# Two expert layers of a perceiver block: totals kept by adding scatters, the shared expert inside routing, the choice in halves

## What is computed

```
# layer 0: E=64 experts, K=6 of them for a token, hidden width 176
s = softmax(x @ gate_w.T); idx = the K largest of s + gate_b; w = s[idx]
# an expert takes its first CAP=128 tokens in token order; later ones are dropped
y[tok] += w * (silu(x[tok] @ w1.T) * (x[tok] @ w3.T)) @ w2.T
y += (silu(x @ ws1.T) * (x @ ws3.T)) @ ws2.T          # shared expert, width 352

# layer 1: 64 experts, TOPK=8 from the best 4 of 8 groups, hidden width 128, no cap
s = sigmoid(x @ w_router); swb = s + b_router
# group score = sum of its two largest swb; swb of other groups is set to 0
idx = the 8 largest; w = 2.5 * s[idx] / (sum(s[idx]) + 1e-20)
y[tok] += w * (silu(x[tok] @ we_gate) * (x[tok] @ we_up)) @ we_down
y += (silu(x @ ws_gate) * (x @ ws_up)) @ ws_down      # shared expert, width 128
```

## Time and profile before

| | us |
|---|---|
| median of 3 runs | 2524.7 (2523.28 to 2529.2) |
| profiled execution | 2530.89 |
| its span | 2529.0 |

### The profile page before, as it was taken

The page is one execution under the profiler, slowest core; times in us unless marked ns, Lnnn a source line. Parts: engine busy times, 40 slices in busy tenths (PEclk is TensorE's granted clock), DMA queues, the critical chain, the costliest instruction groups (busy, mean ns, idle before and its releaser), DMA issues. The chain is left out here.

```text
span 2529.0 us, 40086 instructions
## 1 busy us (share of the span) xinstructions
PE 1946.5 (77%) x11338; PEld 1327.9 (53%) x11339; DVE 1596.9 (63%) x3459; ACT 1052.6 (42%) x3039; POOL 1204.2 (48%) x999
## 2 busy tenths in 40 slices
PE   5699967888887646998868999778635899998410
PEld 5378833343433232775436888567521777776200
DVE  6599818999999867334846777455579333332643
ACT  1367627656574234442027777433215222222000
POOL 1488606766666501774004555255300544453576
PEclk9699988999999955999969999899855899999755
DMA  7211213303030012885421111000040889899333
GB/s 214 79 67 74 99 33 133 108 27 121 14 134 1 0 59 77 264 253 159 126 67 31 35 31 31 27 2 1 26 154 1 255 277 275 276 260 225 104 115 106
DMA packets 163386, 274.38 MB, mean 108 GB/s; under 512 B 28674, under 2 KB 95339, under 8 KB 163060
## 3 DMA queue, kind: packets, MB, share of 16 engines
q1 hardware_dynamic: 108788, 186.31, 23.4%
q0 software_dynamic: 24320, 58.81, 8.9%
q10 hardware_dynamic: 30144, 27.62, 3.2%
HBM read 223.03 MB, written 56.90 MB: 111 GB/s over the span
## 5 line engine op out<-in xcount | busy, mean ns | idle before, releaser
L982 POOL TENSOR_TENSOR b_h<-b_h,b_bcb 128x1024 f32<-128x1024 f32 x128 | 301.8, 2358 | 151.4 <-DVE b_h L1020 150.8
L1406 POOL DMA_INDIRECT m1x_xb<-scratch_xn,m_tok x192 | 181.5, 945 | 334.9 <-PE m1x_psx L1433 166.9
L838 PE MATMUL b_psy<-b_h,ident 128*128 128x512 f32 x512 | 255.0, 625 | 75.2 <-POOL b_h L982 75.1
L1020 DVE TENSOR_TENSOR_SCAN b_h<-b_dA,b_pbx 128x1024 f32<-128x1024 f32 x128 | 292.6, 2286 | 4.4
L1504 DVE TENSOR_TENSOR m1x_hT<-m1x_sg,m1x_psh 128x128 f32<-128x128 f32 x192 | 55.3, 288 | 260.0 <-ACT m1x_sg L1475 260.0
L1444 PE MATMUL m1x_psh<-m1x_xe,m1x_w 128*128 128x128 f32 x1536 | 209.3, 280 | 10.7 <-DMA m1x_w<-in_m_w 10.6
L838 PEld LDWEIGHTS b_psy<-b_h,ident 128*128 128x128 f32 x512 | 94.7, 196 | 218.8 <-POOL b_h L982 130.4
L940 ACT ACTIVATE b_dA<-b_delta,b_A 128x504 f32<-128x504 f32 x256 | 166.8, 706 | 92.9 <-DVE b_h L1020 88.0
L1444 PEld LDWEIGHTS m1x_psh<-m1x_xe,m1x_w 128*128 128x128 f32 x1536 | 190.3, 195 | 15.4 <-DMA m1x_w<-in_m_w 7.2
L1014 DVE TENSOR_TENSOR b_pbx<-b_pdx,b_bcb 128x1024 f32<-128x1024 f32 x128 | 157.6, 1231 | 51.1 <-ACT b_pdx L924 45.1
L1768 POOL TENSOR_TENSOR x_s<-x_s,x_rs 128x1024 f32<-128x1024 f32 x64 | 121.1, 1893 | 133.7 <-DVE x_rs L1935 133.6
(11 more groups left out here) (421 smaller groups left out, 4590.4 us busy)
## 6 DMA issues: line engine op xcount, KB each, us to landing
m1x_w<-in_m_w SPq DMA_DIRECT2D x192, 256.0 KB, 4.4
b_bcb<-scratch_bc_rows SPq DMA_DIRECT2D x64, 512.0 KB, 4.8
scratch_y<-m1x_yb ACTq DMA_DIRECT2D x192, 128.0 KB, 4.2
m0x_w<-in_m_w SPq DMA_DIRECT2D x64, 368.0 KB
scratch_y<-a_clear SPq DMA_DIRECT2D x16, 768.0 KB, 3.2
m0c_yg<-scratch_y SPq DMA_DIRECT2D x16, 768.0 KB, 4.6
a_c<-in_ctxT SPq DMA_DIRECT2D x16, 512.0 KB, 3.7
m0x_w<-in_m_w SPq DMA_DIRECT2D x64, 128.0 KB
```

Source lines behind the costliest of these rows:

```text
L838: mm = pe.matmul(psy[:, k % 2, :], ident[:, :], h[:, u % HB, j, :], start=False, stop=(nq == NQ - 1 and j == CQ - 1))
L982: q.tensor_tensor(hs, hs, bcb[:, 1, CQ * nq:CQ * nq + CQ], ALU.mult).then_inc(sem("hc"), 1)
L1020: v.tensor_tensor_scan(h[:, u % HB].rearrange("p j n -> p (j n)"), dA[:, u % DB].rearrange("p j n -> p (j n)"), pbx[:, :, :].rearrange("p ...
L1406: g.indirect_dma_start(out=xb[:, j, :], out_offset=None, in_=xn, in_offset=bass.IndirectOffsetOnAxis(ap=tok[:, b:b + 1], axis=0)).then_inc ...
```

## The change

Layer 0: the scores are stored behind each row of `xn` (rows of 320 numbers), so that a gathered row carries its token's weights. DVE multiplies a block's output by the row's score for that expert. Instead of a row for each token and choice there are three totals of one row a token (`NSUM` = 3, with 128 spare rows for empty slots); POOL's scatter of block b adds into total b mod 3, and waits until that total's last scatter has landed. The combine adds three totals for four tiles at a time. The first stage clears 6.7 MB in 6 stores. R becomes 16, and the first 16 blocks' weights are loaded during routing. The table carries only the token, DVE writes `atb` for one pair in three, ACT for two.

Both layers: normalized tiles go through a ring of 4, ACT copies a turned tile once, gate products stay in PSUM for all tiles. The choice (`chosen`) is made for 8 tiles and then for the other 8. Units 0 to `SECOND` - 1 of the shared expert (7 of 12, 4 of 4) are computed in routing, the rest in combine. POOL's gather waits for the output of the block R before.

```diff
-    R = 8
+    totals = [d[f"y{layer}{n}"] for n in range(NSUM)] if capped else None
+    R, XR = 16 if capped else 8, 4
+    UNITS = NSB * NG
+    FIRST, SECOND = (2, 7) if capped else (2, 4)
...
+        def shared_products(pe, m, gate, up):
+            g, n = m // NSB, m % NSB
+            for k2, out in enumerate((gate, up)):
+                for k in range(KD):
+                    mm = pe.matmul(out[0:SBW[n]], ws13[:, k, k2, P * n:P * n + SBW[n]], xnT[:, k, GT * g:GT * g + GT],
+                                   start=(k == 0), stop=(k == KD - 1))
+            mm.then_inc(rs("gu"), 1)
+        def shared_gated(v, m, up):
+            g, n = m // NSB, m % NSB
+            w = SBW[n]
+            v.wait_ge(rs("sgs"), m + 1)
+            v.tensor_tensor(hs[0:w, n, GT * g:GT * g + GT], sgs[0:w, m % 2, :], up[0:w], ALU.mult).then_inc(rs("hs"), 1)
...
             def by_scalar(n):
-                return capped or n % ACT3 == ACT3 - 1
+                return n % 3 != 2 if capped else n % 3 == 2
...
+                    for t in range(NT):
+                        sp.wait_ge(rs("xr"), t + 1)
+                        sp.dma_start(xn[P * t:P * t + P, 0:D], xr[:, t % XR, :]).then_inc(rs("xr_stored", t % XR), 16)
+                    if capped:
+                        for j in range(R):
+                            expert_weights(sp, j, j)
+                    else:
+                        sp.dma_start(w2all[:, :, :], d["m1_w2"].rearrange("e f d -> f e d")).then_inc(rs("w2all"), 16)
+                    if capped:
+                        sp.wait_ge(rs("scores"), 2)
+                        sp.dma_start(xn[:, D:D + E].rearrange("(t p) e -> p t e", p=P), sc[:, :, :]).then_inc(rs("scores_stored"), 16)
...
+                    turn(0)
+                    for t in range(1, NT):
+                        turn(t)
+                        logits(t - 1)
+                    logits(NT - 1)
+                    for m in range(FIRST):
+                        units(m)
+                    pe.wait_ge(rs("hs"), FIRST)
+                    for n in range(2):
+                        for k in range(K):
+                            pe.wait_ge(rs("oh"), K * n + k + 1)
+                            for ranks, w in ((psl, ltrib), (pst, onesb)):
+                                mm = pe.matmul(ranks[:, HN * n:HN * n + HN, :], w[:, :], oh[:, HN * n:HN * n + HN, k, :], start=(k == 0), stop=(k == K - 1))
                     mm.then_inc(rs("ranks"), 1)
+                    for m in range(FIRST, SECOND):
+                        units(m)
...
+                    for t in range(XR, NT):
+                        normed(t)
+                    chosen(0)
+                    chosen(1)
...
+                    shared_gated(v, FIRST, gate_up(FIRST)[1])
+                    for n in range(2):
+                        q = slice(HN * n, HN * n + HN)
+                        for k in range(K):
+                            ins = v.tensor_tensor(pr[:, :, k, :], oh[:, q, k, :], sel[:, q, :], ALU.mult)
+                        step(ins)
+                        step(v.tensor_reduce(slotf[:, q, :], pr[:, :, :, :], AX_X, ALU.add))
+                        for m in range(FIRST + 1 + 2 * n, min(FIRST + 3 + 2 * n, SECOND)):
+                            shared_gated(v, m, gate_up(m)[1])
...
+                    step(v.tensor_scalar(tok[:, :], table, -1.0, 0.0, ALU.add, ALU.max))
+                    step(v.tensor_scalar(slotv[:, 0, :], table, 0.0, nodest[:, 0:1], ALU.is_equal, ALU.mult))
+                    step(v.scalar_tensor_tensor(dest[:, :], slotv[:, 0, :], -1.0, table, ALU.add, ALU.add))
...
                     def rows(b):
                         j, n = b % R, b // R
                         if n:
-                            g.wait_ge(xs("xb", j), 16 * n)
-                            g.wait_ge(xs("xb_used", j), n)
+                            g.wait_ge(xs("yb", b % 2), (b - R) // 2 + 1)
+                            if capped:
+                                g.wait_ge(xs("y_added", (b - R) % NSUM), 16 * ((b - R) // NSUM + 1))
...
                     def outputs(b):
-                        j, n = b % R, b // R
+                        s, n = b % NSUM, b // NSUM
                         g.wait_ge(xs("yb", b % 2), b // 2 + 1)
-                        g.indirect_dma_start(out=y, out_offset=bass.IndirectOffsetOnAxis(ap=dest[:, b:b + 1], axis=0), in_=yb[:, j, :],
-                                             in_offset=None, bounds_check=T * K - 1, oob_is_err=False).then_inc(xs("y_stored", j), 16)
+                        if n:
+                            g.wait_ge(xs("y_added", s), 16 * n)
+                        g.indirect_dma_start(out=totals[s], out_offset=bass.IndirectOffsetOnAxis(ap=dest[:, b:b + 1], axis=0), in_=yb[:, b % R, :],
+                                             in_offset=None, compute_op=ALU.add).then_inc(xs("y_added", s), 16)
...
+                            v.tensor_scalar(yb[:, j, :], psyy[u][:, 0:D], xb[:, j, bass.ds(R * p + j + D, 1)], None, ALU.mult).then_inc(xs("yb", u), 1)
...
+                    for g in range(NG) if capped else ():
+                        for s in range(NSUM):
+                            sp.dma_start(yg[:, g, s, :, :], totals[s].rearrange("(t p) d -> p t d", p=P)[:, 4 * g:4 * g + 4, :]).then_inc(cs("yg", g), 16)
...
+                        v.wait_ge(cs("yg", g), 16 * NSUM)
+                        for s in range(NSUM):
+                            v.tensor_tensor(xg, xg, yg[:, g, s, :, :], ALU.add).then_inc(cs("summed"), 1)
+                            v.wait_ge(cs("summed"), NSUM * g + s + 1)
+                        for i in range(t - 3, t + 1) if capped else ():
+                            v.bn_stats(e["stats"][:, i, :], X[:, i, :]).then_inc(cs("next_bn"), 1)
```

More of the change, by code:

```diff
@@ L44 @@
 HB0 = 64
-SLOTS0 = E * CAP0
 NB1 = T * K1 // P + E
-SLOTS1 = NB1 * P
+NSUM = 3
 HK = 16
@@ L247, in stage_mla @@
         oT = sb("oT", [P, 2, 8, P])
-        NCL = 16
-        clear = sb("clear", [P, T * K0 * D // (P * NCL)])
-        y_clear = d["y0"].rearrange("(n p r) d -> n p (r d)", n=NCL, p=P)
+        NCL = 2
+        clear = sb("clear", [P, (T + P) * D // (P * NCL)])
+        y_clear = [d[f"y{layer}{n}"].rearrange("t d -> (t d)").rearrange("(m p f) -> m p f", m=NCL, p=P)[m]
+                   for layer in range(1) for n in range(NSUM) for m in range(NCL)]
         psk = ps("psk", [P, 4, 512])
@@ L1112, in stage_moe @@
             atb = r.sb("atb", [P, HQ, NA], F16)
[L1113 to L1117, removed]
+            psT = [r.ps(f"psT{n}", [P, 512]) for n in range(2)]
             psl = r.ps("psl", [P, NT, E])
@@ L1167, in _ @@
[L1167 to L1173, removed]
+                            mm = pe.matmul(psc[:, t, :], xnT[:, k, P * t:P * t + P], gw[:, k, :], start=(k == 0), stop=(k == KD - 1))
@@ new lines, in logits, with units @@
+                        mm.then_inc(rs("logits"), 1)
+                    def units(m):
+                        pe.wait_ge(rs("shared"), 32)
+                        if m > FIRST:
+                            pe.wait_ge(rs("sel"), 1)
+                        if m >= 2 and m != FIRST:
+                            pe.wait_ge(rs("hs"), m - 1)
+                        shared_products(pe, m, *gate_up(m))
+                    turn(0)
+                    for t in range(1, NT):
+                        turn(t)
+                        logits(t - 1)
@@ L1290, in _ @@
-                    for t in range(NT):
-                        ins = v.max(top[:, t, :], sel[:, t, :])
-                    step(ins)
-                    for t in range(NT):
-                        ins = v.max_index(topi[:, t, :], top[:, t, :], sel[:, t, :])
-                    step(ins)
-                    step(v.tensor_copy(topf[:, :, :], topi[:, :, :]))
-                    for k in range(K):
-                        v.tensor_tensor(oh[:, :, k, :], bc(iota[:, None, :], NE), bc(topf[:, :, k:k + 1], NE), ALU.is_equal).then_inc(rs("oh"), 1)
+                    step(v.memset(before[:, 0, :], 0.0))
```

430 lines of the change are left out of this document (208 added, 222 removed).

## The result

The changed kernel takes 2489.5 us (median of 4 runs, 2484.0 to 2490.9), the kernel before 2525.7 beside it. The ratio is 0.9852, 95% interval 0.9832 to 0.9871: 36 us faster. The forecast was 2469, range 2457 to 2506, so the direction and the range hold and the size is 20 us short.

A forecast was written before the change was run, and what follows sets the result against it. Bounds before: PE in both expert loops, DVE in both routings and the first combine, POOL in the last. Terms summed to -55.7 us, 2530.9 to 2475.2 profiled, less 6.2 to the median: 2469, range 2457 to 2506.

The forecast's parts named there:

- The experts of layer 0, the adding scatter: Layer 0 experts: POOL's adding scatter taken at 1.02 us, like a plain one, upper bound 2.0; no cost.
- rival A: Layer 0 experts: POOL becomes the bound through a longer adding scatter, +13 at 1.5 us, +45 at 2.0; chance 0.14.
- B: Layer 0 experts: the three chains of additions pace blocks mildly, landing 8.1 to 10.6 us, +18 at 9; chance 0.15.
- The step to the median, -6.2: Whole kernel: the profiled execution lay 6.2 us above the runs' median; the same difference was taken off 2475.2.
- The landing of the adding scatter, 6.5 taken: Layer 0 experts: an adding scatter lands in 6.5 us, free up to 8.1 with three totals; effect 0.
- C: Layer 0 experts: chains of additions make the kernel slower than before, landing 10.8 us or more, up to +69; chance 0.06.
- Borders of rounds, -1.5: Layer 0 experts: four rounds instead of eight save half of the excess at the borders of rounds, -1.5 us.
- Combine of layer 0, -44.6: Layer 0 combine: less DVE work makes PE the bound, 47.8 us instead of 92.4, -44.6.
- Routing of layer 0, -7.2: Layer 0 routing: shorter table loop -10.0, tail -1.0, gated products +3.3, halves' overhead +0.5; sum -7.2 us.
- Rival D: Routing: shared units stay at 1.2 GHz and DVE waits for them, +11 us in layer 0, +4 in layer 1; chance 0.08.
- Layer 1: Layer 1: routing -1.2 us, bounds -4 and +4; experts 0; combine 0.
- First stages: First stage: 6 clears for 16, behind DVE and PE, 0 us.

The follow-up runs named there:

- e1: The changed kernel with plain scatters in layer 0's experts, the addition in the transfer left out: 2470.8 us, ratio 0.9754.
- e2: The changed kernel with six totals instead of three, the combine reading only three of them: 2491.1 us, ratio 0.9841.
- e8: The changed kernel with each adding scatter taking only rows 0 to 63 of the block's 128: 2497.4 us, ratio 0.9624.
- e12: The kernel before with only layer 0's expert rings changed, 16 blocks in four rounds instead of 8 in eight: 2527.8 us, ratio 0.9994.
- e4: The changed kernel with nine of layer 0's shared units in routing instead of seven, and three gated products after each half's slots instead of two: 2496.0 us, 0.9863.
- e7: The changed kernel with eight shared units in layer 0's expert loop, four in routing, none in combine, gated products regrouped: 2488.9 us, ratio 0.9590.
- e9: The changed kernel with seven shared units in routing, five in layer 0's expert loop, none in combine, gated products regrouped: 2497.1 us, ratio 0.9618.

## Why the prediction was right in direction and 20 us off

*The experts of layer 0, the adding scatter: "I take 1.02".* This is the step that failed: a term mis-sized. The bounds on record were 1.02 and 2.0, the value taken the lower end because of the same 128 rows of 1 KB. It measured 1.58, and with 0.28 us a block to spare that made POOL the bound. This is rival A, priced at 13 us for 1.5 and 45 for 2.0; 1.58 put into the same sum (0.97 + 1.58 + 0.54 = 3.09 a block) gives +18, and the loop came out 17.9 us above the forecast (+16.4 for -1.5). e1 takes the addition out: its loop is 20.2 us shorter, its time 20.3 below e2's on the same chip, and 0.9754 of 2524.7 is 2463, inside the forecast's own range of 2460 to 2478. "The same rows, the same kind" was the wrong argument, since e8 shows that the rows hardly count. The measured time lies outside that range of its own and inside the wide one only because the wide one had been drawn to take in rivals A and B.

*The step to the median, -6.2.* The sum gave 2475.2 for a profiled execution, and that measured 2490.9, 15.7 more. The other 5 us of the miss come from taking off the 6.2 by which the profiled execution of the kernel before lay above its median; that of the changed kernel lay 1.4 above.

*The landing of the adding scatter, 6.5 taken.* It measured 6.0, 7.6 at most, below the 8.1 that three totals allow. Rivals B and C did not come. The estimate of 3.9 to 5.7 that was worked out there from the Trainium skill, "DMA: Bandwidth & Descriptors", on latency, lies a little low. In e1 the plain scatter lands in 5.6, so the addition is worth about 0.4, with a DMA share of 0.99 against 0.86 beside it (1010 to 1160). The other 1.9 us over the 3.7 of before are not the DMA share, which was 0.89 in the same window of the kernel before. What else is new in e1 (all 128 rows stored, other targets, no bound on the indices) was not tried apart. The DMA load over the whole stage, forecast to stay or grow a little, went from 0.79 of 197 us to 0.89 of 213, 156 to 190 engine-us, above the 172 that was its upper figure.

*Borders of rounds, -1.5.* Right in kind, and short. ScalarE's lines in the old loop (the kernel before, window 985 to 1212) have two table loads in each of the seven rounds that are a loop in the program:

```profile
L1469 ACT ACT_TABLE_LOAD x7 | 9.0, 1283 | 7.5 <-PE m0x_psx L1433 7.5
L1475 ACT ACT_TABLE_LOAD x7 | 9.0, 1283 | 0.1
```

e12 has three such rounds with the same pair in each, and is 2.1 us shorter; the changed kernel has none at all, and e1's loop is 173.5, which is 63 x 2.755 to 0.1. So all of the excess went, not half (3.5 us by the prediction's rounded pace, 3.7 by the two profile times); shared among the pairs it is 0.5 us each in the old loop (7) and in e12 (1.6 us over, 3). That the loads and not the borders themselves cost this is argued from e1, whose loop has three borders and no load. Why the new loop has no such loads was not tried.

*Combine of layer 0, -44.6.* 1195.2 to 1243.5 is 48.2 us for 92.4: -44.2. PE is the bound as said, the first eight matmuls take 6.14 us where 3.43 + 2.1 was allowed, the tail after the last product is DVE's (7.0 us, 7.6 forecast). e4 takes two units of PE's work out and 6.5 us go. Ahead of the stage, from the last turn to its start, it is 15.9 us for 13.1, where +1.5 was forecast.

*Routing of layer 0, -7.2.* The table loop took 20.3 us for a forecast of 20.1. To the first gather -9.6: 2.4 better, most of it at the ranks, which came 51.7 us after the stage's start and not 54.0 (the forecast had them where they were). Rival D, units that don't fit beside DVE, was not true at seven (DVE waits for no silu there) and is at nine (e4, 5.55 us). The first block came 3.7 us after its gather, 3.2 forecast.

*Layer 1.* Routing to first turn -2.6 for -1.2, the loop -2.6 for 0, the end +1.2 for 0. None of these was tried by itself. *First stages:* 2.4 earlier; but in the other runs with the same first stages the routing starts at 881.5 to 887.4, and in the two of the old kernel at 881.2 and 883.3, so this is what executions differ by.

## What to carry to other kernels

An engine at 90% of the pace is nearly the bound. When its transfers get a new flag, here the addition, the time of the instruction that issues them may change as well as their landing, and both need a term. Where the trace has no row for it and the bounds are far apart (here 1.02 and 2.0 us), compare them with the slack (here 0.28 us a block): most of that range lay beyond it, and 14 in 100 was too little for it. When another engine takes over as the bound, the old one has slack, and work of it that stands alone elsewhere can move in: in e7, 28 us of matmuls cost the loop 7 to 8 and took 15 off the combine. And where a run carries a second edit, as e4's grouping, another run must show that edit apart: without e9 its 3.9 us would pass for a lack of room on PE.

## What the runs showed of the hardware that was not expected

- An indirect scatter of 128 rows of 1 KB that adds holds POOL 1581 ns, a plain one 989 (1018 in the kernel before, with a bound on the indices), a gather 973 to 989. With 64 rows the adding one still takes 1465.
- Its landing is hardly longer than that of a plain one in the same kernel: 6.0 against 5.6 us (medians), at a DMA share of 0.99 against 0.86.
- The same kernel takes 2525 to 2531 us in three groups of runs and 2594 in two others, on other chips, with its loop over layer 0's experts 32 us longer on the one that was profiled; the changed kernel's differs by 2 us.
- Two ScalarE table loads of 1283 ns stand at each round of the old loop, and it is 0.5 us a round longer than its pace gives; the new loop has neither.
